# A two-layer graph network on one core: VectorE's order, the order of transfers and the shape of stores in the last stage

## The reference

```python
def sage(h, src, dst, deg_inv, W_self, W_neigh, b):
    agg = segment_sum(h[src], dst, num_segments=1250)
    return h @ W_self + (agg * deg_inv[:, None]) @ W_neigh + b
h1 = relu(sage(x2, ..., W_self0, W_neigh0, b0))
y = sage(h1, ..., W_self1, W_neigh1, b1)
out = layernorm(x2 + y)          # over 1024 columns
```

## Time and profile before

| | us |
|---|---|
| Median of 3 runs (1079.29 to 1082.65) | 1082.34 |
| The profiled execution | 1082.9 |
| Its span, first to last instruction or transfer | 1080.8 |
| The last stage, from its first job at 402.66 | 678.1 |
| TensorE busy | 965.1 (89%) |
| VectorE busy | 735.2 (68%) |
| ScalarE busy | 451.9 (42%) |
| GpSimd busy | 217.7 (20%) |

### The profile page before, as it was taken

The page is one execution under the profiler, slowest core; times in us unless marked ns, Lnnn a source line. Parts: engine busy times, 40 slices in busy tenths (PEclk is TensorE's granted clock), DMA queues, the critical chain, the costliest instruction groups (busy, mean ns, idle before and its releaser), DMA issues.

```text
span 1080.8 us, 14336 instructions
## 1 busy us (share of the span) xinstructions
PE 965.1 (89%) x4630; PEld 768.7 (71%) x4630; DVE 735.2 (68%) x1716; ACT 451.9 (42%) x864; POOL 217.7 (20%) x328
## 2 busy tenths in 40 slices
PE   5798898989899998888999998998998999998893
PEld 3376678978788886666777766776766777776672
DVE  7877866465668876767746777633778857787743
ACT  5677743242534776323423333433343313333322
POOL 3000012841532420223020222010121011121000
PEclk9699999999999998989999999999999999999997
DMA  5257783992103864556483645364343384434653
GB/s 200 60 92 207 180 188 74 213 205 56 39 22 130 280 233 140 162 161 153 120 264 129 185 127 137 120 192 140 105 155 111 95 312 163 150 123 153 204 187 124
DMA packets 62306, 164.51 MB, mean 152 GB/s; under 512 B 19523, under 2 KB 20532, under 8 KB 62030
## 3 DMA queue, kind: packets, MB, share of 16 engines
q0 software_dynamic: 18688, 71.90, 24.1%
q1 hardware_dynamic: 33198, 71.64, 23.0%
q10 hardware_dynamic: 10336, 19.85, 5.0%
HBM read 133.09 MB, written 56.02 MB: 175 GB/s over the span
## 4 chain that ended last, share of the span: by engine, by line
PE 50%; DVE 21%; issue 9%; ACT 8%; DMA 6%; POOL 1%; ACTq 1%; DVEq 0%; POOLq 0%
PE bank L2130 17%; PE bank L2114 15%; PE bank L1120 5%; PE bank L1152 4%; PE bank L666 3%; DVE h_stage L1880 3%; DMA w_piece<-w_neigh 2%; ACT h_stage L1749 2%; DMA t_dram<-w_piece 2%; PE bank L630 2%; DVE w_piece L1969 2%; DVE w_slot L1980 2%; DVE hot_keys L447 2%; DMA w_piece<-t_dram 2%; ACT squares L1347 2%
## 5 line engine op out<-in xcount | busy, mean ns | idle before, releaser
L2114 PE MATMUL bank<-w_slot,h_stage 128*125 128x512 f32 x1680 | 410.7, 403 | 34.1 <-DVE h_stage L1880 23.2
L2114 PEld LDWEIGHTS bank<-w_slot,h_stage 128*125 128x125 f32 x1680 | 314.0, 189 | 128.7 <-DVE h_stage L1880 40.2
L2130 PE MATMUL bank<-g_rows,a_stage 125*125 125x512 f32 x800 | 191.0, 398 | 11.0 <-issue 10.9
L2130 PEld LDWEIGHTS bank<-g_rows,a_stage 125*125 125x125 f32 x800 | 148.3, 187 | 51.4 <-issue 14.6
L1782 ACT ACTIVATE w_slot<-w_piece 128x512 fp32r<-128x512 f32 x104 | 64.9, 630 | 192.3 <-DVE w_piece L1969 91.1
L2031 DVE SCALAR_TENSOR_TENSOR o<-bank,deg_inv,o 125x512 f32<-125x512 f32 x40 | 30.0, 751 | 96.8 <-PE bank L2130 96.8
L1685 POOL DMA_DIRECT2D w_piece<-w_neigh x80 | 44.3, 567 | 244.5 <-DMA t_dram<-w_piece 129.3
L1152 PE MATMUL bank<-a_turned,gn 125*128 125x418 f32 x360 | 70.8, 354 | 3.9 <-DVE gn L1012 2.9
L1152 PEld LDWEIGHTS bank<-a_turned,gn 125*128 125x128 f32 x360 | 66.9, 188 | 5.7 <-DVE gn L1012 3.5
L1980 DVE TENSOR_TENSOR w_slot<-w_piece,w_slot 128x512 fp32r<-128x512 f32 x104 | 70.3, 683 | 0.0
L1880 DVE TENSOR_TENSOR h_stage<-h_turned,h_stage 128x500 fp32r<-128x500 f32 x60 | 40.3, 676 | 42.8 <-ACT h_stage L1749 42.8
(11 more groups left out here) (236 smaller groups left out, 1336.7 us busy)
## 6 DMA issues: line engine op xcount, KB each, us to landing
a_stage<-at_dram SPq DMA_DIRECT2D x40, 625.0 KB, 6.3
w_piece<-w_neigh POOLq DMA_DIRECT2D x80, 256.0 KB, 3.4
w_piece<-w_self POOLq DMA_DIRECT2D x56, 256.0 KB, 3.7
t_dram<-w_piece ACTq DMA_DIRECT2D x32, 256.0 KB, 2.4
w_piece<-t_dram POOLq DMA_DIRECT2D x32, 256.0 KB, 3.1
at_dram<-a_turned SPq DMA_DIRECT2D x10, 625.0 KB, 10.1
dec_y<-x_bd SPq DMA_DIRECT2D x10, 512.0 KB, 4.2
dec_x<-x_ob SPq DMA_DIRECT2D x10, 512.0 KB, 4.5
```

The costliest lines, as they stand in the source:

```text
L2114: mm = pe.matmul(bank(q, i)[0:NT, :], st[m % 3][:, a, k, :], slots[w % 3][:, b, k, :], start=(k == 0 and p == 0), stop=(k == HK - 1 and p ...
L2130: mm = pe.matmul(ps_a[u][0:NT, :], cast(a_st[t % 3][0:NT, k, :]), cast(g[0:NT, h, k, :]), start=(n == 0 and h == 0), stop=(n == T - 1 and ...
```

## The change

It has five parts, all in `sage_block`. (1) VectorE's order in `at_job`: join, eviction, weight_low, stage_low, weight_sums, then the sums of node blocks; some of these move to other jobs, and so do sets 3, 5 and 6. In quarter 0 the first sums use a buffer of their own. (2) t1 is not stored and loaded: set 6 loads its two pieces again and VectorE subtracts them a second time. The stores of t2 count on two semaphores by turns, and a piece of set 3 is free when VectorE has used it. (3) The bias additions go from one for each set w = 4 to 13 to one behind each slice k of sets 7, 8 and 9. (4) SP asks for counts of tile 2 ahead of the loads for x2 or y, and for those of tile t + 1 ahead of the rows of tile t. (5) Transfers of 125 rows of h1, y and the output become one of 120 rows and one of 5; the output goes out in whole rows of 4 KB, for which ScalarE writes both normalized halves into res.

```diff
     PLACE = {job: i for i, job in enumerate(JOBS)}
-    PIECES = (1, 1, 1, 3, 2, 2, 1)
+    PIECES = (1, 1, 1, 3, 2, 2, 2)
...
     RING = 5
+    ROWS = ((0, 120), (120, NT))
...
     piece_in = [sem(f"piece_in{n}") for n in range(RING)]
-    (w_sum, SUM0), (w_hi, HI0), (w_lo, LO0), (t_out, OUT0) = s.spent[0:4]
+    (w_sum, SUM0), (w_hi, HI0), (w_lo, LO0) = s.spent[0:3]
+    t_out = [s.spent[3], s.spent[18]]
...
     temp = [tile_at(f"s_temp{n}", [128, HK, NT], F32, s.rows_at + 4096 + 2016 * n) for n in range(2)]
+    first_temp = tile_at("s_first", [128, HK, NT], F32, s.dec_at + 2048 * (HT + 9))
...
     def sum_order(w, k):
         q, i = divmod(w, SETS)
-        return 16 * q + {3: 2 * k, 4: 8 + k, 5: 12 + k}[i]
+        return 20 * q + {3: 2 * k, 4: 8 + k, 5: 12 + k, 6: 16 + k}[i]
     def pieces_until(w, k):
...
     def out_count(q, u):
-        return 16 * HT * (0, 1, 1, 2)[q]
+        return 32 * HT * (0, 1, 1, 2)[q]
     def nodes_known(eng, q, t):
...
     def quarter_sets(q, i):
-        when = ((2, (2, 3, 4, 5)), (3, (6, 8, 10, 12))) if q == 0 else ((3, (5, 7, 9, 12)),)
-        when += ((4, (13, 14, 15, 16)), (5, (20, 21, 22, 23)), (6, (24, 25, 26, 27)))
+        when = ((2, (2, 3, 4, 5)), (3, (6, 8, 10, 12))) if q == 0 else ((3, (5, 7, 9, 11)),)
+        when += ((4, (13, 14, 15, 16)), (5, (18, 19, 20, 21)), (6, (23, 25, 27, 28)))
...
     def tile_sets(q, t):
...
                 sp.wait_ge(turned, t - 1)
-            sp.dma_start(rows[u][0:NT, :], io["h1_dram"][t, 0:NT, 0:512]).then_inc(rows_in[u], 16)
+            for p0, p1 in ROWS:
+                sp.dma_start(rows[u][p0:p1, :], io["h1_dram"][t, p0:p1, 0:512]).then_inc(rows_in[u], 16)
         def load_x2(t):
...
             for t in range(4 * n, min(4 * n + 4, T)):
-                sp.dma_start(res[t][:, 0, :], io["x2_dram"][t, :, 512:D]).then_inc(both_in[n][0], 16)
-                sp.dma_start(res[t][0:NT, 1, :], io["y_dram"][t, 0:NT, :]).then_inc(both_in[n][0], 16)
+                sp.dma_start(res[t][:, 1, :], io["x2_dram"][t, :, 512:D]).then_inc(both_in[n][0], 16)
+                for p0, p1 in ROWS:
+                    sp.dma_start(res[t][p0:p1, 0, :], io["y_dram"][t, p0:p1, :]).then_inc(both_in[n][0], 16)
...
                 load_rows(1)
+            load_counts(q, 2)
...
             for t in range(2, T):
-                load_counts(q, t)
+                if t + 1 < T:
+                    load_counts(q, t + 1)
...
     def _(pool):
         def load(n, source):
             pool.dma_start(piece[n % RING][:, :], source).then_inc(piece_in[n % RING], 16)
+
+        def wait_spill(q, k):
+            landed, base = t_out[k % 2]
+            pool.wait_ge(landed, base + 16 * (2 * q + k // 2 + 1))
         def freed(n):
...
                         continue
-                    if w % SETS == 3 and j in (0, 2):
-                        pool.wait_ge(t_out, OUT0 + 32 * (HK * (w // SETS) + k + 1))
-                    if j == 1:
+                    if w % SETS == 3 and j == 2:
+                        wait_spill(w // SETS, k)
+                    if w % SETS == 3 and j == 0:
+                        pool.wait_ge(w_sum, SUM0 + sum_order(w, k) + 2)
+                    elif j == 1:
                         pool.wait_ge(w_sum, SUM0 + sum_order(w, k) + 1)
-                    elif not (w % SETS == 3 and j == 0):
+                    else:
...
             if i == 5:
-                pool.wait_ge(t_out, OUT0 + 32 * HK * (q + 1))
-            if 0 <= w - 4 < T:
-                pool.wait_ge(*s.x2_landed[w % 2])
-                pool.dma_start(io["x2_dram"][w - 4, :, :], io["sage_b"][1:2, :].to_broadcast([128, D]),
-                               accum_op=ALU.add).then_inc(x2_biased, 16)
+                wait_spill(q, 2)
+                wait_spill(q, 3)
...
                 b11, b12, b21, b22 = w_self[k], w_neigh[k], w_self[HK + k], w_neigh[HK + k]
-                t1, t2 = io["t1_dram"][q, k], io["t2_dram"][q, k]
-                sources = ((b11,), (b21,), (b22,), (b12, b11, b22), (b22, b12), (b21, t2), (t1,))[i]
+                t2 = io["t2_dram"][q, k]
+                sources = ((b11,), (b21,), (b22,), (b12, b11, b22), (b22, b12), (b21, t2), (b12, b11))[i]
...
                     load(n, source)
+                tile = HK * (w - SETS) + k
+                if 0 <= tile < T:
+                    pool.wait_ge(*s.x2_landed[tile % 2])
+                    pool.dma_start(io["x2_dram"][tile, :, :], io["sage_b"][1:2, :].to_broadcast([128, D]),
+                                   accum_op=ALU.add).then_inc(x2_biased, 16)
     def piece_of(eng, w, k, j):
...
                 act.wait_ge(p_done, NJ * before + HT * last + HT)
-            if i in (3, 4, 5):
+            if i in (3, 4, 5, 6):
...
             if i == 3:
-                act.dma_start(io["t1_dram"][q, k], piece[pieces_until(w, k) % RING][:, :]).then_inc(t_out, 16)
-                act.dma_start(io["t2_dram"][q, k], source[:, :]).then_inc(t_out, 16)
+                act.dma_start(io["t2_dram"][q, k], source[:, :]).then_inc(t_out[k % 2][0], 16)
         def at_job(q, i):
...
             for j, t in enumerate(own):
-                for y in (res[t][0:NT, 1, :], o[t][0:NT, :]):
-                    act.activation(y, y, ACT.Identity, bias=f_sh[n % 2][0:NT, j:j + 1], scale=f_rs[n % 2][0:NT, j:j + 1])\
-                       .then_inc(f_normed, 1)
+                for h, y in enumerate((res[t][0:NT, 0, :], o[t][0:NT, :])):
+                    act.activation(res[t][0:NT, h, :], y, ACT.Identity, bias=f_sh[n % 2][0:NT, j:j + 1],
+                                   scale=f_rs[n % 2][0:NT, j:j + 1]).then_inc(f_normed, 1)
                 act.wait_ge(f_normed, NORMED0 + 2 * t + 2)
-                act.dma_start(io["out"][t * NT:(t + 1) * NT, 0:512], res[t][0:NT, 1, :]).then_inc(o_out[t % 2], 16)
-                act.dma_start(io["out"][t * NT:(t + 1) * NT, 512:D], o[t][0:NT, :]).then_inc(o_out[t % 2], 16)
+                for p0, p1 in ROWS:
+                    act.dma_start(io["out"][t * NT + p0:t * NT + p1, :], res[t][p0:p1, :, :].rearrange("p h d -> p (h d)"))\
+                       .then_inc(o_out[t % 2], 16)
         def finish(q, t):
...
             if q == 0:
-                act.dma_start(io["h1_dram"][t, 0:NT, 0:512], o[t][0:NT, :]).then_inc(o_out[u], 16)
+                for p0, p1 in ROWS:
+                    act.dma_start(io["h1_dram"][t, p0:p1, 0:512], o[t][p0:p1, :]).then_inc(o_out[u], 16)
             if q == 2:
-                act.dma_start(io["y_dram"][t, 0:NT, :], o[t][0:NT, :]).then_inc(o_out[u], 16)
+                for p0, p1 in ROWS:
+                    act.dma_start(io["y_dram"][t, p0:p1, :], o[t][p0:p1, :]).then_inc(o_out[u], 16)
...
         def first_sums(q, r):
             nodes_known(dve, q, HT + r)
+            sum1 = first_temp if q == 0 else temp[r % 2]
             if q == 0:
-                dve.wait_ge(*s.x2_landed[1])
-                dve.wait_ge(*s.x2_turned[1])
-            if r >= 2:
+                dve.wait_ge(*s.y_products)
+                dve.wait_ge(sums[2], r)
+            elif r >= 2:
                 dve.wait_ge(sums[2], HT * q + r - 1)
-            elif q > 0:
+            else:
                 dve.wait_ge(st_ready, NJ * q)
-            dve.tensor_tensor(temp[r % 2][:, :, :], ht[:, 0:HK, cols(HT + r)], ht[:, HK:KD, cols(HT + r)], ALU.add)\
+            dve.tensor_tensor(sum1[:, :, :], ht[:, 0:HK, cols(HT + r)], ht[:, HK:KD, cols(HT + r)], ALU.add)\
...
             dve.wait_ge(sums[1], 2 * HT * q + r + 1)
-            dve.tensor_tensor(s2[r][:, :, :], temp[r % 2][:, :, :], ht[:, 0:HK, cols(r)], ALU.subtract).then_inc(sums[2], 1)
+            dve.tensor_tensor(s2[r][:, :, :], sum1[:, :, :], ht[:, 0:HK, cols(r)], ALU.subtract).then_inc(sums[2], 1)
         def fourth_sum(q, r):
...
                 dve.wait_ge(sums[2], HT * (q + 1))
+                if q == 0:
+                    dve.wait_ge(*s.x2_landed[1])
+                    dve.wait_ge(*s.x2_turned[1])
...
         def weight_sums(w, k):
             i = w % SETS
-            if not made(w) or i not in (3, 4, 5):
+            if not made(w) or i not in (3, 4, 5, 6):
...
         def at_job(q, i):
+            if PLACE[7, 0] < i <= PLACE[7, HT - 1] + 1:
+                join(q, i - 1 - PLACE[7, 0])
...
                 evict(q, i - 1)
-            if i + 2 < NJ:
-                stage_low(q, i + 2)
-            start = 3 if q == 0 else 0
-            if start <= i < start + HT:
-                first_sums(q, i - start)
-            if 7 <= i < 7 + HT:
-                fourth_sum(q, i - 7)
-            if i in (13, 14, 18, 19, 20):
-                third_sum(q, (13, 14, 18, 19, 20).index(i))
-            if 17 <= i < 17 + HT:
-                join(q, i - 17)
-            if i in (23, 24, 28, 29, 30):
-                first_sum_again(q, (23, 24, 28, 29, 30).index(i))
-            if i > NJ - HT + 1:
-                g_low(q, i - 2 - NJ + HT)
...
                     weight_low(w, k)
```

(21 more changed lines are left out.)

## The result

| | before | after |
|---|---|---|
| Median of 4 runs each, us | 1082.49 (1079.29 to 1084.25) | 1021.86 (1019.73 to 1025.21) |
| The profiled execution, us | 1082.9 | 1019.73 |
| Its span, us | 1080.8 | 1017.8 |

The change makes the kernel faster: ratio 0.9446, 95% interval 0.9411 to 0.948, 60.6 us by the medians, where 45.5 were forecast. The direction was right; 1021.86 lies just under the low end of the range, 1022, and 15 us under the forecast.

The account below looks back on a forecast made before the run. TensorE, nearly always busy, was taken to wait mainly for VectorE's late stages and weights. From 1082.3 us, -15.5 +7 -6 -6 -7 -6 -5 -7 = -45.5 gave 1036.8, forecast 1037, range 1022 to 1054.

Parts of the forecast that it names:

- Rival A: VectorE still paces, ScalarE and VectorE waiting on each other; half of the products' 34.5 us lost: 1054 us, chance 0.13.
- The terms -15.5, -6, -7, -6: Forecast changes in us for the block products of quarters 0, 1, 2 and 3.
- I take 6, 7 and 6 us of the rest, leaving 1 to 3 us each: Products of quarters 1 to 3: gains taken from losses of 8.8, 14.9 and 8.6 us.
- the hand layout: Quarter 0's products, new order laid out by hand: 2 us of waits and 1 of clock remain, 15.5 gained.
- counted operations over jobs 18 to 30: VectorE's spread load after moving sets: 55 operations, 33.0 us, fit within 13 products, 36.4 us.
- So an addition takes 4.9 us with pieces at 0.71 and 3.5 with pieces at 0.87; I take 4.2.: DMA engine time of one bias addition into x2, from GpSimd's queue in 448 to 470 us.
- the +7: First aggregation: moved bias additions overfill the DMA engines by 10.5 us, 9 taken as stall against 2.3 now.
- rival C: First aggregation: the bias additions are hidden, +0 or +1 instead of +7: 1030 us, chance 0.12.
- B: First aggregation: additions starve a_stage, +11 instead of +7, and late pieces cost another 4: 1045 us, chance 0.15.
- D: Slower: additions hold the engines as long as they take to land; 1075 us at 8.3 us each, chance 0.03.
- Last aggregation -5.3 for -5: Quarter 3: SP's earlier counts of tile 2 remove a 3.48 us wait and 1.6 of clock, -5 us.
- Rival E: The split does nothing, 125 and 120 rows behaving alike: 1044 us, chance 0.05.

Follow-up runs that it names:

- e1_order: The changed kernel with VectorE's old order inside a job (stage_low behind the eviction, weights last), operations kept in their new jobs: 1047.09 us.
- e8_turn: The changed kernel with the last turn of h1 in quarter 2 ahead of job 1 instead of behind it: 1016.76 us.
- e9_places: The changed kernel with sets 3, 5 and 6, the joins and the repeated first sum in their old jobs, new order inside a job kept: 1031.66 us.
- e7_twice: The changed kernel with each bias addition issued twice, the second into a scratch DRAM tensor that nothing reads: 1047.83 us.
- e4_sp_order: The changed kernel with SP's old order, counts behind h1's rows and behind the loads of x2 or y: 1026.31 us.
- e3_nosplit: The changed kernel with transfers of 125 rows again, whole output rows of 4 KB kept: 1032.29 us.
- e5_spill: The changed kernel with t1 stored and loaded again, and pieces 0 and 2 of set 3 waiting for the stores: 1031.77 us.
- e6_before_split: The kernel before with only the split into 120 and 5 rows and the whole output rows: 1068.16 us.

## Why the prediction came out as it did

**The bound and the order.** Right in kind: VectorE's late stages and weights were what TensorE waited for, and with the subtraction in the gap the waits for h_stage went from 23.2 to 5.9 (6 expected) and those for w_slot to none. e1_order shows that the order inside the job is the largest part, 25 of 60.6 us, and 21.1 of the 44.8 in the products; no run separates the filled gap from the earlier weights. Rival A, VectorE still paces, is out.

**The size in the products.** This is the larger part of the miss: of the 17.8 us by which the stages above beat the forecast (15.1 by the medians) it makes 10.3, and the first aggregation 6.2. The terms -15.5, -6, -7, -6 measured -18.3, -8.3, -10.1, -8.2. The step that failed is "I take 6, 7 and 6 us of the rest, leaving 1 to 3 us each", for which no row was given, and the 3 us that the hand layout kept in quarter 0. Next to nothing was left. In quarter 0 the hand layout had 2 us of waits at jobs 9, 11, 13 and 15; the trace has one, 0.36 us at job 9. In quarters 1 and 3 I kept 2.8 and 2.6 us and 0.5 is left. In quarter 2 I kept 7.9 and 4.8 is left, almost all of it the 5 behind the last turn of h1. The losses that I divided were lengths less a count at full clock, so the slower clock was in them, and I never split it off. By the busy columns the 44.8 us are 29.6 of idle time and 15.2 of TensorE's own busy time. Where waits go the granted clock rises, 0.95 to 0.97, 0.97 to 0.98 and 0.98 to 1.00 in quarters 0, 2 and 3, and the busy time there falls by 5.5, 4.3 and 3.3 us. e8_turn is the direct evidence: 2.7 us of waits taken away were worth 4.7.

**The jobs to which sets moved.** The step counted operations over jobs 18 to 30 as a gain. e9_places shows none of it in three quarters: the new order inside the job was enough. The gain of quarter 3 is there but comes from elsewhere, from how set 6's pieces fall against SP's loads.

**The first aggregation.** The other step that failed. "So an addition takes 4.9 us with pieces at 0.71 and 3.5 with pieces at 0.87; I take 4.2." It was a term of the sum, 74 us of transfers against 63.5, that was mis-sized, and with it the +7. GpSimd's queue takes 44.8% of 48 us, 21.5, for 5 additions and 10 pieces; pieces alone take 41.4% of 25 us for 3.08 MB, 0.88 each; so an addition is (21.5 - 8.8)/5 = 2.5 us. e7_twice gives (52.9 - 8.8)/16 = 2.8 by its share (11.01 MB less ten pieces are sixteen additions' bytes) and 2.8 by its time. An a_stage is 36.1% of 48 over nine, 1.93. With 2.8 and 0.88 the same nine additions, twelve pieces, nine a_stages and the stores (11.5% of 48, 5.5) are 25 + 11 + 17 + 6 = 59 us, under the 63.5, and nothing overflows: +0.8 as in rival C. The two values came from one window with one addition in it and eight pieces, and the addition got the whole remainder. I took the middle; the lower end, with the pieces' price that is now measured, would have given 3.5 and a sum of 68, still 4 over.

**Rivals B and D.** B has the right mechanism at twice the load. e7_twice shows that the excess goes mostly to what stands behind the additions in their own queue (18.6 us more at quarter 1's first job), and less to a_stage on another (7.1). D, an addition holding the engines for as long as it takes to land, is out: in after the additions land 12.1 us after the issue, and take 2.5.

**SP's order, the last aggregation, the split and the tail.** Second aggregation -6.9 for -6: e4_sp_order gives 5.4 of it back, and without the split (e3_nosplit) it stays at 54.2. Last aggregation -5.3 for -5, right in sum by luck: I laid all of it to SP's order, which alone gives 2.9, and counted nothing there for the split, which alone gives 3.8. Tail -7.0 for -7, for the reason given. Rival E is out by e3_nosplit.

**t1 recomputed** was priced inside the products, its stores at nothing; e5_spill puts the part at 9.9 us. Taken back one at a time the parts are 25.2 (order), 9.9 (t1), 10.4 (split), 9.8 (places), 4.5 (SP) and 1.3 (additions). That this comes to 61 is no proof that they add: the split alone on the kernel before gave 13.7 where its removal costs 10.4.

Open: why an addition takes 3.5 us in the earlier trace rows even with pieces at 0.87, and 2.5 to 2.8 here. What the buffer of its own for quarter 0's first sums is worth; it is in after and in no kernel taken away. Whether e9_places' late pieces are due to the DMA engines being full or to the pieces' turn among queues; no run separates these. Why the third aggregation waits 0.9 to 1.2 us in e4_sp_order and e6_before_split, and neither before nor in after. In quarter 1 the busy time fell by 2.0 at a granted clock that reads 1.00 in both, and no run says why. How the split shortens the last aggregation was not looked at transfer by transfer.

## What to carry to other kernels

In a stage whose engines run in step, look for the gap that an engine has in each turn and put into it the work that others wait for longest; move its place in the turn before moving it to another turn. When waits of an almost full TensorE go, count the clock behind each of them as well. Price a transfer from a stretch where its queue carries nothing else, and list what stands behind it in its own queue before asking what shares the engines.
